# Fewer, wider one-hot operations in the routing stage of an attention and mixture-of-experts kernel, and an earlier split of the second expert's input

## The reference

```python
def reference(x, ctx_1024, ...):
    # attention layer: a gated linear attention of x over ctx, 8 batches x 128 tokens x 128 features, 8 heads
    x = x + _L0_xattn_ref(_layernorm(x), ctx_1024, ctx_1024, igate_w, igate_b, fgate_w, fgate_b, ln_scale)
    # expert layer over the same 1024 tokens
    x = x + _L0_ffn_ref(_layernorm(x), expert_tokens, W1, b1, W2, b2, W3, b3)
    return x

def _L0_ffn_ref(x, expert_tokens, W1, b1, W2, b2, W3, b3):   # 8 experts, 128 -> 512 -> 512 -> 128
    scores = einsum('bnd,ed->bne', x, expert_tokens)
    _, topk_idx = top_k(scores, 2)
    outputs = zeros_like(x)
    for i in range(8):
        w = mean(topk_idx == i, axis=-1, keepdims=True)      # 0.5 for a token that chose expert i, else 0
        h = gelu(x @ W1[i] + b1[i], exact); h = gelu(h @ W2[i] + b2[i], exact)
        outputs = outputs + (h @ W3[i] + b3[i]) * w
    return outputs
```

## Time and profile before

| | before |
|---|---|
| median of 3 runs | 167.78 us (167.64 to 170.52) |
| the profiled execution, device time | 168.79 us |
| its span, first to last instruction | 167.0 us |
| mean granted TensorE clock | 0.986 of full speed |
| busy: PE / VectorE / ScalarE / GpSimd | 90% / 74% / 65% / 63% of the span |

### The profile page before, as it was taken

The page is one execution under the profiler, slowest core; times in us unless marked ns, Lnnn a source line. Parts: engine busy times, 40 slices in busy tenths (PEclk is TensorE's granted clock), DMA queues, the critical chain, the costliest instruction groups (busy, mean ns, idle before and its releaser), DMA issues.

```text
span 167.0 us, 3194 instructions
## 1 busy us (share of the span) xinstructions
PE 150.7 (90%) x1026; PEld 127.7 (76%) x1030; DVE 123.4 (74%) x374; ACT 108.9 (65%) x239; POOL 104.6 (63%) x128
## 2 busy tenths in 40 slices
PE   7999959999999997993999999999999999999900
PEld 2496326676769755892999999999999999999900
DVE  0889469697979977999895977959959779572400
ACT  3276497465638645781987988969889699656100
POOL 7799200002139588997678878788687770838480
PEclk9999999999999999999999999999999999999995
DMA  4679503999999920000102213223131030122230
GB/s 139 143 235 378 155 13 74 353 368 368 370 363 366 266 81 16 0 0 0 35 22 36 26 32 35 28 33 30 37 30 27 22 31 6 16 28 19 20 38 7
DMA packets 19210, 17.72 MB, mean 106 GB/s; under 512 B 2136, under 2 KB 13880, under 8 KB 19192
## 3 DMA queue, kind: packets, MB, share of 16 engines
q1 hardware_dynamic: 15408, 15.21, 28.1%
q0 software_dynamic: 3392, 2.18, 11.0%
q10 hardware_dynamic: 392, 0.10, 0.5%
HBM read 14.70 MB, written 2.69 MB: 104 GB/s over the span
## 4 chain that ended last, share of the span: by engine, by line
PE 70%; POOL 13%; DVE 6%; issue 3%; ACT 2%; DMA 2%; POOLq 1%; SPq 1%; DVEq 0%
PE bank L1386 42%; PE bank L1247 9%; PE bank L1213 5%; POOL dec L447 5%; POOL ohb L445 3%; PE bank L1155 3%; PE bank L1233 2%; PE bank L1443 2%; PE bank L1232 2%; POOL out_rows L520 2%; DMA RH<-parts 2%; PE bank L1375 1%; POOL qm L439 1%; DVE qm L804 1%; POOLq L69 1%
## 5 line engine op out<-in xcount | busy, mean ns | idle before, releaser
L520 POOL DMA_INDIRECT out_rows<-ys,ids x24 | 38.3, 1597 | 17.3 <-DVE ys L1081 9.0
L1386 PE MATMUL bank<-g1h,whi 128*128 128x304 f32 x128 | 39.5, 309 | 0.0
L1386 PE MATMUL bank<-g1l,whi 128*128 128x304 f32 x128 | 38.6, 302 | 0.0
L1386 PE MATMUL bank<-g1h,wlo 128*128 128x304 f32 x128 | 38.5, 301 | 0.0
L715 ACT ACTIVATE g<-bank,smt 128x304 f32<-128x304 f32 x63 | 31.3, 520 | 10.3 <-PE bank L1386 10.3
L863 DVE TENSOR_TENSOR wlo<-wraw,whi 128x512 fp32r<-128x512 f32 x48 | 30.8, 687 | 1.8 <-ACT whi L627 1.5
L627 ACT ACTIVATE whi<-wraw 128x512 fp32r<-128x512 f32 x48 | 28.1, 652 | 1.3 <-PE bank L1311 1.3
L507 POOL DMA_INDIRECT xg<-xn_rows,ids x18 | 22.1, 1228 | 6.7 <-issue 4.6
L1386 PEld LDWEIGHTS bank<-g1h,whi 128*128 128x128 f32 x128 | 24.1, 188 | 0.2 <-issue 0.2
L1386 PEld LDWEIGHTS bank<-g1h,wlo 128*128 128x128 f32 x128 | 24.1, 189 | 0.0
L1386 PEld LDWEIGHTS bank<-g1l,whi 128*128 128x128 f32 x128 | 24.1, 188 | 0.0
(11 more groups left out here) (212 smaller groups left out, 320.8 us busy)
## 6 DMA issues: line engine op xcount, KB each, us to landing
wraw<-in_L_ffn_W SPq DMA_DIRECT2D x8, 1024.0 KB, 9.1
wraw<-in_L_ffn_W SPq DMA_DIRECT2D x16, 256.0 KB, 8.8
xs<-in_x SPq DMA_DIRECT2D x2, 256.0 KB, 3.4
cs_in<-in_ctx SPq DMA_DIRECT2D x2, 256.0 KB, 4.9
out_rows<-cs_in SPq DMA_DIRECT2D x8, 64.0 KB, 2.6
xn_rows<-qn SPq DMA_DIRECT2D x8, 64.0 KB, 2.5
out_rows<-ys,ids POOLq DMA_INDIRECT x24, 3.3
xg<-xn_rows,ids POOLq DMA_INDIRECT x18, 2.8
```

What stands on the lines that cost most here:

```text
L520: g.indirect_dma_start(out=out, out_offset=bass.IndirectOffsetOnAxis(ap=ids[0:n, col:col + 1], axis=0), in_=ys[0:n, e % 2, c, :], in_offse ...
L1386: last = t.matmul(dst, wcol(w, p, layer, k, m), act_(k), start=(n == 0), stop=(n == 3 * (1 if layer == 1 else MC) - 1))
```

## The change

Four things change.

- GpSimd makes only the column one-hots (`oha`) of batches 0 to 3, 8 operations and not 16, and waits for `cf` instead of `rf` before them.
- VectorE makes all 16 row one-hots in two `tensor_tensor` operations of 8 x 128 elements per partition. Both inputs are read with repeats: `iotab` along the middle dimension, `rf` along the innermost.
- VectorE makes the 8 column one-hots of batches 4 to 7 in one `tensor_tensor` of 8 x 72 elements, and multiplies them by `tokval` in another of 4 x 144, in place, after a wait on the first. These four operations take the place of 16 `tensor_scalar` operations. TensorE's waits in `lists` follow.
- For expert 1's input, ScalarE's `round_x(1)` and VectorE's `low_x(1)` come behind the first piece of that expert's weights instead of the fifth.

```diff
 # GpSimd
             def onehots(b):
-                pool.wait_ge(s.listing_pool, 12)
+                pool.wait_ge(s.listing_pool, 10)
                 for n in range(2):
-                    g.tensor_scalar(ohb[:, 2 * b + n, :], iotab[:], rf[:, b, n:n + 1], None, ALU.is_equal)\
-                        .then_inc(s.onehots_pool, 1)
                     g.tensor_scalar(oha[:, 2 * b + n, :], iotab[:, 0:NC], cf[:, b, n:n + 1], tokval[:, b:b + 1],
                                     ALU.is_equal, ALU.mult).then_inc(s.onehots_pool, 1)
 # ScalarE
                 if e + 1 < NE:
                     weights_hi(e + 1, 1)
+                    if e == 0:
+                        round_x(1)
...
                     weights_hi(e + 1, 2)
-                    if not late:
+                    if e >= 1 and not late:
                         round_x(e + 1)
 # VectorE
-            def onehots(b):
-                dve.wait_ge(s.rf_done, 1)
-                for n in range(2):
-                    v.tensor_scalar(ohb[:, 2 * b + n, :], iotab[:], rf[:, b, n:n + 1], None, ALU.is_equal)\
-                        .then_inc(s.onehots_dve, 1)
-                    v.tensor_scalar(oha[:, 2 * b + n, :], iotab[:, 0:NC], cf[:, b, n:n + 1], tokval[:, b:b + 1],
-                                    ALU.is_equal, ALU.mult).then_inc(s.onehots_dve, 1)
+            def onehots():
+                for half, ready, count in ((0, s.listing_pool, 12), (1, s.rf_done, 1)):
+                    rows = rf[:, 4 * half:4 * half + 4, :].rearrange("p b n -> p (b n)")
+                    dve.wait_ge(ready, count)
+                    v.tensor_tensor(ohb[:, 8 * half:8 * half + 8, :], iotab[:].unsqueeze(1).to_broadcast([128, 8, 128]),
+                                    rows.unsqueeze(2).to_broadcast([128, 8, 128]), ALU.is_equal).then_inc(s.onehots_dve, 1)
+                cols = cf[:, 4:8, :].rearrange("p b n -> p (b n)")
+                v.tensor_tensor(oha[:, 8:16, :], iotab[:, 0:NC].unsqueeze(1).to_broadcast([128, 8, NC]),
+                                cols.unsqueeze(2).to_broadcast([128, 8, NC]), ALU.is_equal).then_inc(s.onehots_dve, 1)
+                marks = oha[:, 8:16, :].rearrange("p (b n) c -> p b (n c)", n=2)
+                dve.wait_ge(s.onehots_dve, 3)
+                v.tensor_tensor(marks, marks, tokval[:, 4:8].unsqueeze(2).to_broadcast([128, 4, 2 * NC]), ALU.mult)\
+                    .then_inc(s.onehots_dve, 1)
...
-            for b in range(4, B):
-                onehots(b)
+            onehots()
             count_tokens()
...
                     weights_lo(e + 1, 1)
+                    if e == 0:
+                        low_x(1)
                     weights_lo(e + 1, 2)
-                    if not late:
+                    if e >= 1 and not late:
                         low_x(e + 1)
 # TensorE
                 if b < 4:
-                    pe.wait_ge(s.onehots_pool, 4 * b + 4)
+                    pe.wait_ge(s.onehots_pool, 2 * b + 2)
+                    pe.wait_ge(s.onehots_dve, 1)
                 else:
-                    pe.wait_ge(s.onehots_dve, 4 * (b - 4) + 4)
+                    pe.wait_ge(s.onehots_dve, 4)
```

## The result

| | before | after |
|---|---|---|
| median of 20 runs | 168.68 us (167.62 to 170.76) | 167.66 us (167.31 to 170.68) |
| ratio | | 0.9949, 95% interval 0.9928 to 0.9970 |
| span of the profiled execution | 167.0 us | 165.4 us |
| mean granted TensorE clock in it | 0.986 | 0.989 |

The changed kernel is faster by 0.5%, and the interval lies clear of 1; the medians of the twenty are 1.02 us apart. The ratio is taken over fast executions alone, which leaves out those more than 1.5% above the fastest of their kernel. A difference of 0.5% is far under 2%. The three runs of the kernel before that were known ahead had a lower median (167.78) than the twenty (168.68).

A forecast was written before the change was run, and what follows sets the result against it. TensorE's matmul chain bounds, stalled by GpSimd's one-hots, with VectorE's queue nearly as late behind. Gain 1.43 us less 0.53 us queue growth is 0.90 us; 167.78 - 0.9 = 166.9 us, range 166.0 to 168.4 us.

The forecast's parts named there:

- The stall: TensorE's 2.83 us wait in `lists`: would vanish, about 1.9 us turning into smaller waits on VectorE.
- the last k-step: In the first quarter of expert 1's layer 2 on TensorE: would start near 82.59 instead of 83.49, gaining 0.90 us.
- the sum: Whole kernel: the 0.9 us gain taken off the median of the runs, 167.78 us, giving 166.9 us.
- The price of the wide operations: VectorE's four wide one-hot operations: 3.80 us against 3.27 us for 16 small ones, so its queue grows 0.53 us.
- The bound of 2.0 us from half the price an element: VectorE's wide operations at half price: 2.04 us, queue 1.2 us shorter; chance 0.07 together with winning the full stall.
- The rule of gain: At expert 1's layer 2 on TensorE: gain is 1.43 us less whatever VectorE's queue grows by.
- The moved input split: Expert 1's input: earlier order delays nothing in sum; left behind the fifth piece, TensorE would have stood for 1.5 us.
- GpSimd's end: GpSimd's eight column one-hots: done near 70.6, or 71.8 with the slowest row, before TensorE asks at 75.28.
- the rival in which GpSimd's running operation holds VectorE up: First two wide operations wait behind GpSimd's: VectorE loses 1.15 us more, gain -0.25, 168.0 us; chance 0.10.
- The gather: Expert 2's third gather: issued at 83.35, landed at 86.15, 0.5 us before TensorE's transpose; late-gather rival 167.6 us, chance 0.09.
- The step behind it: Whole kernel, chances against no change: within 2% (3.4 us) 0.93, faster 0.03, slower 0.04.

The follow-up runs named there:

- the first comparison: The changed kernel against the kernel before, 20 runs each: medians 167.66 us against 168.68 us, ratio 0.9949.
- the fp16 experiment: The changed kernel with the row numbers kept as fp16, so both inputs and the output of the wide row one-hots are fp16: 167.75 us.
- three kernels: The changed kernel with one wide row one-hot operation more (169.18 us), the token count later (167.38 us), or VectorE's one-hots made one by one (168.22 us).
- the later sets: Experiment sets that ran the kernel before again, unchanged: medians 171.43; 172.17 and 171.53; 170.77; 169.42 and 170.27 us.
- the third set: The changed kernel and the kernel before run again, both unchanged: 167.62 us against 170.77 us, ratio 0.990 (0.986 to 0.994).
- the two cases tried: The changed kernel with the input split moved back, 167.98 us; and with VectorE's queue shortened, `read_lists` early 166.86 us or left in place 166.54 us.

## Why the prediction was right in size and wrong in what it said of it

- **The stall goes where it was said.** The 2.83 us wait went, VectorE's queue took its place, and the last k-step came at 82.42 us, predicted 82.59. The gain at that landmark was 1.07 us, 0.10 of it from ahead of `lists`; 0.90 was predicted. In the first comparison the ratio gives a gain of 0.5%; 0.90 of 167.78 us is 0.5% too.
- **A step that failed is the sum**: "against the median: 167.78 - 0.9 = 166.9". The 0.90 us held; the 167.78 did not. It was the median of three runs, and that of twenty was 168.68, close to the profiled execution (168.79) from which the gain had been read. From 168.68 the same sum gives 167.8, 0.1 from the measured 167.66. The prediction moved its result 1.0 us down to the three runs without asking why the profiled one lay above them. Against that execution it gave a span of 166.1 us and 1.79 outside; measured were 165.4 and 2.07.
- **The price of the wide operations**: 3.77 us measured, 3.80 worked out from two other sizes. The bound of 2.0 us from half the price an element is excluded by this measurement, and for fp16 row numbers too by the fp16 experiment.
- **The rule of gain**, 1.43 us less the growth of the queue: confirmed one to one at the landmark by three kernels. Measured, the constant is 0.97 + 0.50 = 1.47.
- **The moved input split** was costed at nothing lost and, had it stayed, at a wait of 1.5 us "right there". The wait was 1.19 us, and the sentence suggests a worth that the move does not have beside the wide one-hots: the queue would have absorbed it. That followed from my own reading and I didn't draw it. What the move does to GpSimd's one-hots in the kernel before (a wait of 1.89 us instead of 2.83) was not foreseen at all.
- **GpSimd's end** was put at 70.6 to 71.8; it was 72.64. Its longest one-hot took 3.0 us beside the wide operations, which took 1.155 us each where 1.17 was worked out. So the rival in which GpSimd's running operation holds VectorE up did not occur, and the opposite did, hidden by 2.5 us of slack.
- **The gather** was issued when predicted (83.36 against 83.35) and was not late, even with the landmark 1 us earlier.
- **The step behind it failed too, from the sum to the chances.** The argument gave a gain with few ways around it, but I set 2% as what a measurement can tell from no change and gave 0.93 to "within 2%", which says no more than that nothing large would come. The measurement resolved 0.2%: 0.9928 to 0.9970. The forecast should have said faster, by 0.5%.
- **And one effect was put at nothing.** I read the granted clock as 1.00 in one execution and took the standstill to cost its own length. In the later sets two of three executions of the kernel before had a mean clock under 0.98; in the trace that caught the drop it cost another 1.54 us at the landmark. No rival covered it; the page's mean clock of 0.986 for one execution could not show it, but the spread of the three runs (167.64 to 170.52) was a hint that I left aside. That the ratio of the first comparison came out at the predicted size although this was left out is in part luck: it was 0.990 in the third set. How much of the 168.68 us is owed to the drop is not shown, as no clocks are on record for those twenty.

## What to carry to other kernels

When a stall on the tensor engine is removed, read the queue of the next engine in it: the gain is the stall less what that queue still makes it wait. Inside that queue the amount of work counted here, and in the two cases tried (`low_x`, `read_lists`) not its order. But an order that is free for its own engine can change the pace of another, as the 0.84 us one-hot of GpSimd shows. Merging small vector operations saved 0.6 us of 4.4 here, and fp16 did not make the merged form with its repeated operand cheaper. A standstill of 2 to 3 us on the tensor engine may cost more than itself, in some executions, since the clock can fall behind it; look at the mean granted clock over many runs, not at one trace. And take a gain off the time of the execution in which it was read.

## What the runs showed of the hardware that was not expected

- With a standstill of 1.89 to 2.88 us in an otherwise busy stretch, TensorE's granted clock fell to 0.50 in three of five traces: 0.8 us and 0.2 us after it was busy again, and once 0.7 us before. It stayed there for 3.4, 3.4 and 6.8 us. By their mean clock 85 of 128 executions of the kernel before lay under 0.98, and 1 of 24 with that time filled by matmuls whose results nobody reads.
- GpSimd's one-hot of 72 elements took 0.60 us at the shortest and 3.0 us beside two-input operations of 1024 elements on VectorE, which came every 1.155 us. Four 512-element ones came every 0.60 us with GpSimd idle (74.53 to 76.94 in the changed kernel) and five every 0.612 us beside GpSimd's one-hots in the kernel before.
- `tensor_scalar` operations of one kind on 128 fp16 elements follow each other every 0.17 us, alternating with ones that have two scalar operands every 0.19 (2.98 us for 16, from 70.63 to 73.61).
